# Last network: the load of the next block's addresses directly behind a block's four set products

## What is computed

```python
x1 = x_nodes[src].reshape(-1, 16, 32)
x2 = x_edges.reshape(-1, 16, 32)
i1, i2, i3 = (path_indices[:, 0], path_indices[:, 1], path_indices[:, 2])
contrib = path_coeffs[None, :, None] * x1[:, i1, :] * x2[:, i2, :]
edge_out = zeros.at[:, i3, :].add(contrib)
out = zeros.at[dst].add(edge_out.reshape(-1, 512))
```

## Time and profile before

| | |
|---|---|
| median of three runs | 902.3 us |
| the profiled execution, its own time | 895.13 us |
| its span | 893.3 us, granted TensorE clock 0.954 of full speed |
| busy over the span | TensorE 87%, VectorE 68%, ScalarE 26%, GpSimd 16% |
| last network | from about 559 us; groups at 575.6, 622.9, 684.6, 748.8, 813.0; sums to x from 877.5 |
| chain that ended last, by engine | PE 33%, issue 32%, DVE 23%, DVEq 7%, POOL 2%, others 1% or less each |

### The profile page before, as it was taken

The page is one execution under the profiler, slowest core; times in us unless marked ns, Lnnn a source line. Parts: engine busy times, 40 slices in busy tenths (PEclk is TensorE's granted clock), DMA queues, the critical chain, the costliest instruction groups (busy, mean ns, idle before and its releaser), DMA issues.

```text
span 893.3 us, 10417 instructions
## 1 busy us (share of the span) xinstructions
PE 777.2 (87%) x2858; PEld 499.2 (56%) x2858; DVE 607.8 (68%) x1579; ACT 230.4 (26%) x460; POOL 139.3 (16%) x149
## 2 busy tenths in 40 slices
PE   6688898898898999999999997188979995996998
PEld 2345465455466657657558563176566582582673
DVE  8774675675684533533633544288999999999895
ACT  6522122123122321321321221401602403403300
POOL 6000000000001000000010001741261261240000
PEclk9889999999999999999999999599999997997999
DMA  6813214323331333333233100671541452330000
GB/s 203 293 40 114 102 55 150 106 79 121 106 118 40 121 111 113 106 112 112 105 112 107 59 0 23 192 227 51 169 139 47 142 142 71 100 113 0 0 1 23
DMA packets 39653, 89.93 MB, mean 101 GB/s; under 512 B 3986, under 2 KB 4255, under 8 KB 39615
## 3 DMA queue, kind: packets, MB, share of 16 engines
q1 hardware_dynamic: 34496, 72.71, 24.3%
q0 software_dynamic: 5120, 16.78, 6.4%
HBM read 88.43 MB, written 1.05 MB: 100 GB/s over the span
## 4 chain that ended last, share of the span: by engine, by line
PE 33%; issue 32%; DVE 23%; DVEq 7%; POOL 2%; ACT 1%; DMA 1%; POOLq 0%; ACTq 0%; SPq 0%
PE PS L744 23%; DVE big L1446 6%; PE PS L1003 5%; DVE tail L1437 5%; DVEq L1416 3%; DVE tail L1456 2%; DVE prods L1456 2%; PE PS L753 2%; DVEq L1420 1%; POOL rstd L537 1%; DVEq L1446 1%; POOL big L557 1%; DVE h L1088 1%; PE PS L840 1%; PE PS L777 1%
## 5 line engine op out<-in xcount | busy, mean ns | idle before, releaser
L744 PE MATMUL PS<-big 128*128 128x512 f32 (+1 forms) x368 | 137.6, 525 | 2.5 <-DVE big L1350 1.8
L1437 DVE SCALAR_TENSOR_TENSOR tail<-big,coef 128x448 f32 (+3 forms) x216 | 132.3, 615 | 0.0
L1446 DVE TENSOR_TENSOR big<-big,tail 128x448 f32 (+3 forms) x216 | 120.8, 559 | 12.1 <-DVE tail L1437 11.4
L744 PEld LDWEIGHTS PS<-big 128*128 128x128 f32 x368 | 67.3, 190 | 67.0 <-issue 57.9
L537 POOL TENSOR_TENSOR rstd<-var,minus_half 128x1 f32<-128x1 f32 x36 | 29.2, 812 | 439.0 <-DVE var L1062 436.9
L557 POOL DMA_INDIRECT big<-h_rows,src_i x64 | 81.0, 1266 | 82.7 <-PE PS L1003 60.9
L744 PE MATMUL PS<-hT,big 128*128 128x256 f32 x384 | 86.6, 386 | 4.2 <-ACT hT L666 4.2
L744 PEld LDWEIGHTS PS<-hT,big 128*128 128x128 f32 x384 | 73.5, 193 | 16.0 <-issue 3.9
L1003 PE MATMUL PS<-big,hotd_more 128*128 128x512 f32 x176 | 76.5, 592 | 0.0
L1088 DVE TENSOR_TENSOR h<-PS,h 128x512 f32<-128x512 f32 x26 | 17.9, 687 | 74.1 <-PE PS L744 74.1
L1017 PE MATMUL PS<-xn,tail 128*128 128x256 f32 x120 | 32.3, 417 | 33.1 <-DVE tail L1456 33.1
(11 more groups left out here) (196 smaller groups left out, 1074.9 us busy)
## 6 DMA issues: line engine op xcount, KB each, us to landing
big<-in_edge_attr_dram SPq DMA_DIRECT2D x32, 512.0 KB, 3.6
big<-in_L_gnn_vn_W_dram SPq DMA_DIRECT2D x12, 1024.0 KB, 5.3
big<-in_L_gnn_m_w_dram SPq DMA_DIRECT2D x8, 1024.0 KB, 5.2
big<-in_L_gnn_gcn_W_dram SPq DMA_DIRECT2D x7, 1024.0 KB, 5.2
big<-in_L_gnn_wv_dram SPq DMA_DIRECT2D x4, 1024.0 KB, 5.3
big<-in_L_gnn_wq_dram SPq DMA_DIRECT2D x4, 1024.0 KB, 5.4
big<-in_L_gnn_wk_dram SPq DMA_DIRECT2D x4, 1024.0 KB, 5.4
big<-in_L_gnn_wo_dram SPq DMA_DIRECT2D x4, 1024.0 KB, 5.3
```

Source lines behind the costliest of these rows:

```text
L744: return pe.matmul(o, lhsT, rhs, start=start, stop=stop)
L1437: dve.scalar_tensor_tensor(out=prod[:, slot, tiles, :], in0=xs[:, tiles, bass.ds(i1, EXT)], scalar=coef[:, row:row + 1], in1=xe[:, tiles, ...
L1446: dve.tensor_tensor(o, o, prod[:, slot, tiles, :], ALU.add)._wait_ge(path_step, max(product_at[slot], added_at[0])).then_inc(path_step, 1)
```

## The change

In a block with a set, the additions that still wait are now made ahead of the set (in pairs, one behind the other) and the load of the next block's addresses stands directly behind the set's four products; it no longer stands behind row 5. In a group's first block nothing waits, and the load comes ahead of the zeroing. Blocks without a set keep theirs. The number of loads, products and additions stays the same.

```diff
@@ -1474,11 +1474,15 @@
                     behind = block_behind(g, at)
                     has_set = k >= SETS - SETS_OF[g]
                     if has_set:
+                        while waiting:
+                            add_product(*waiting.pop(0))
                         set_rows(k, rows)
+                        if behind is not None:
+                            loaded = load_block(behind)
                     if at == 0:
                         dve.memset(part[SUM_AT[g]][:, 0:ZERO_CUT[0], :], 0.0).then_inc(acc_zero, 1)
                     if g == GROUPS - 1 and at >= len(ORDER[g]) - 2:
-                        if behind is not None:
+                        if behind is not None and not has_set:
                             loaded = load_block(behind)
                         split += [(BLOCK_ROWS * k + i, rows[i]) for i in range(4 if has_set else 0, BLOCK_ROWS)]
                         continue
@@ -1486,7 +1490,7 @@
                         if at == 0 and i == 6:
                             dve.wait_ge(acc_zero, (g + 1) * 3)
                         summed_row(BLOCK_ROWS * k + i, every, *rows[i])
-                        if i == 5 and behind is not None:
+                        if i == 5 and behind is not None and not has_set:
                             loaded = load_block(behind)
```

## The result

Timed in turns with the kernel before on one chip, the changed kernel takes 897.98 us (median of 5, 897.36 to 898.5) where the kernel before takes 903.98 (median of 5, 902.26 to 905.46). The ratio is 0.9932 with a 95% interval of 0.9916 to 0.9948: faster by 0.7%, 6.1 us by the ratio and 6.0 by the medians. The forecast was 898.5 us and a gain of 3.8 us. The time fell where it was forecast partly by chance, since the kernel before came out 1.7 us above the median that I had started from; what has to be explained is a gain of 6.0 where the steps gave 3.8.

The account below looks back on a forecast made before the run. VectorE's queue, stalled by 1602 ns address loads, was taken to leave 33 holes of 11.4 us. Group 0 -0.6, groups 1 to 3 -2.3, group 4 -0.9: -3.8 from 902.3 gives 898.5 us, range 894.3 to 902.4.

Parts of the forecast that it names:

- Step (c): Load behind a set's four products: starts 0.74 us after the pair's first addition; exposed 0.45 (10 tiles), 0.11 (12), hidden (14).
- Step (d): First blocks: the load ahead of the memset delays it by 0.36 us in group 0, nothing with 14 tiles.
- Step (e): Group 4: additions move into VectorE's wait for TensorE, third set's product +0.36 us, fifth set 0.84 late; -0.9 in all.
- who waits for what: Later sets come about 1.2 us later behind two more additions; in group 2 at worst 0.2 us comes of it.
- B: Rival: the queue runs ahead of the flush and every load is hidden; -7.9 us, 894.4 us, chance 0.17.
- C: Rival: slower, the load behind a flush begins only with the set's fourth product; 926 us, chance 0.07.
- D: Rival: the queue needs a step longer, 0.22 us more in 8 blocks of group 0; -1.4, 900.9 us, chance 0.14.

Follow-up runs that it names:

- before_again: The kernel before, unedited, run and profiled a second time: 894.10 us, ratio 0.9989 to the kernel before.
- after_again: The changed kernel, unedited, run and profiled a second time: 889.83 us, ratio 0.9934 to the kernel before.
- before_third: The kernel before, unedited, profiled a third time: 895.63 us, ratio 1.0003 to the kernel before.
- first_as_before: Against the changed kernel, the load in the five first blocks put back behind row 5: 890.39 us, ratio 0.994 to the kernel before.
- after_third: The changed kernel, unedited, profiled a third time: 889.52 us, ratio 0.9942 to the kernel before.
- the flush alone: Against the kernel before, waiting additions made ahead of the set, load left behind row 5: 887.17 us, ratio 0.9903; again 886.48 us, 0.9916.

## Why the prediction was right, and where it was off

**The mechanism held.** VectorE's queue standing still at the load was the cost, and a load behind a flush begins when the four products have been issued and not before. Blocks of 14 tiles went from 6.99 to 6.84 us (forecast 6.8), the holes left are the ten forecast, and the pair ahead of each set is there. By part, before_again against after_again: group 0 -1.1 (forecast -0.6), groups 1 to 3 -0.8, -0.6 and -0.7, together -2.1 (-2.3), group 4 -1.1 (-0.9), in all -4.3 for -3.8.

**The level was chance.** The forecast carried over 7.2 us between the profiled execution and the median of the runs shown, and no run explains that term. In the three later comparisons the kernel before took 895.3 to 895.7 us, close to its profiles, and the changed kernel 889.8 and 889.5: a gain of the same size, but not the 898.5 us, and below the range of 894.3 to 902.4. Range and forecast hold for the first comparison alone. A gain of 4.3 us, what the stages show, would also have lain just under the 4.5 that I had put as the limit of what can be told from none.

**Sizes.** Step (c) put the load's start 0.08 late and so the exposure at 0.45 for 0.38: seven blocks, half a microsecond. Step (d) put the memset at +0.36 for +0.60, since it allowed 0.05 between the load's end and the memset where it takes 0.28. The rest of group 0's difference lies in blocks of the kernel before that took up to 5.90 us where I had counted 5.78. Step (e), in after_again, VectorE in group 4:

```profile
841.58 1.96 DVE L1456 TENSOR_TENSOR tail<-big 128x384 f32 x4 [1.33 <-PE PS L1017]
843.83 1.15 DVE L1437 SCALAR_TENSOR_TENSOR tail<-big,coef 128x384 f32 x2 [0.28 <-issue]
...
853.99 1.96 DVE L1456 TENSOR_TENSOR tail<-big 128x384 f32 x4
856.64 0.75 DVE L1437 SCALAR_TENSOR_TENSOR tail<-big,coef 128x192 f32 x2 [0.69 <-issue]
```

Behind the wait for TensorE the product comes 2.25 us after the set begins, 0.37 more than four steps (forecast 0.36); the fifth set's is 2.65, 0.77 more (forecast 0.84). TensorE's idle time ahead of the split's first half went from 1.49 to 0.43 us (forecast 0.6):

```profile
864.09 7.13 PE L1003 MATMUL PS<-big,xn 128*128 128x512 f32 x16 [0.43 <-DVE big L1446]
```

**What I missed** is in the paragraph on who waits for what. I had looked for a margin that the later sets might lose to TensorE and wrote "at worst 0.2"; in truth the later sets win one. In the kernel before the third set of group 3 had no margin against TensorE in the profile that I had, and that profile was a lucky one: where TensorE starts slowly, the kernel before pays about 1.6 us (before_third: 319.5 for 317.8), 1.06 of them in group 3, where the changed kernel has 1 us of room. In group 4 both wait for TensorE, and the changed kernel pays too: first_as_before, with a start of 9.74 there for 9.35, takes 79.58 for 79.22. Against before_third the stages of after_third give -5.8, but that compares a slow start with a fast one; the three timings gave, by their ratios, -6.1, -5.9 and -5.2 us. That most of the timed runs of the kernel before look like before_third isn't shown: only one of its profiles does. So 4.3 us of the gain are accounted for, up to 1 more is plausible, and the rest is of the size by which two timings of the kernel before differ (1.5 us).

**The rivals.** B, every load hidden, would have given 7.9 and is refuted by the holes of 0.31 behind each set of group 0; its price is what the flush alone brings (8.3 by the stages), which I could have seen: I had noted that the first blocks hide their load behind a run without waits, and a flush with the load left behind row 5 makes such a run in every block. The rule of the Trainium skill (Perfetto Trace Analysis, DVE / Act Engine Instruction) that stood beside it, by which the sequencer goes on once an instruction is in the wait queue, isn't borne out here: the load began at 593.70, 0.66 us after the addition waited for had ended. C is refuted by the load at 593.70, 0.22 behind the set's first product. D had its load 0.22 later than mine; it came 0.08 earlier. The chances were 0.52 for no change and 0.41 for faster, and the timed gain of 0.7% fell to the second.

## What to carry to other kernels

A register load on an engine's own queue costs the engine the load's time (here 1.60 us) less the work that is issued ahead of it without a wait; the queue's own address copies between that wait and the load count against it as well. So count from the last instruction that waits, and collect the waiting instructions in front of that run instead of moving the load closer to its start. When a profile names a releaser on the same engine that had long been done, or a semaphore that had long been reached, look at the queue's own instructions for that line. And before summing a change up from one profile, look for places where an engine passes a wait with nothing to spare: it cost nothing in one execution here and a microsecond in another.

## What the runs showed of the hardware that I hadn't expected

- **The slow stretch.** In one profile of fourteen VectorE's queue took about 0.7 us for address steps that take 0.08 otherwise, from 581 to 593 us, while edge rows and gathers were moving; VectorE's datapath ran at its usual speed (0.49 for a product), and it cost 7 us. The load that falls into it is recorded with 0.73 us instead of 1.60. None of the later profiles, of whatever kernel, has such a stretch, so the runs that held the transfers back test nothing about it. In the first comparison both kernels ran some 8 us slower than in the three later ones, which would fit a stretch in each of those runs: the profiled execution of the changed kernel, with the stretch, is one of its five timed ones, and the five lie within 1.2 us. The profile of the kernel before has none, but at 895.13 us it lies 7 us below that kernel's timed runs and says nothing of them. Both this and the cause stay open.
- **A memset behind a load starts late**: 0.28 us after the load's end, with two address steps of later products in between, where a product starts 0.16 after it (595.31 to 595.47), with one. That the memset waits for those steps isn't tested.
- **TensorE's first 16 multiplications after 6 to 9 us of idling** took 9.14 us in one execution and 10.19 in another of one and the same kernel, with the granted clock over the stretch at 0.77 and 0.69. Over all profiles they took 8.65 to 10.19 at the start of group 3 or 4, and 7.13 where TensorE had idled for less than 2 us.
- **The flush costs no more between sets than at a group's end**: the pair takes 1.27 to 1.28 us with 14 tiles and 1.01 to 1.02 with 10.
